# A four-layer graph network on one core: one-hot tiles and first-hop messages shared with ScalarE, whole-row loads in a Chebyshev pass, and a zero row per partition

## What is computed

```python
# layer 0: attention diffusion, 4 heads, 5 hops
att = segment_softmax(leaky_relu(s_h + s_t + s_r), head_ids)
Z = broadcast(x[:, None, :])                      # [N, 4, 64], every head begins with x
for _ in range(5):
    Z = segment_sum(0.9 * att[:, :, None] * Z[tail_ids], head_ids) + 0.1 * x[:, None, :]
out = Z.reshape(N, 256) @ W_o
# layer 1: four GCN rounds, each with its own norm
# layer 2: Chebyshev, K = 3
def prop(t): return segment_sum(w[:, None] * t[col], row)
T1 = prop(x);  T2 = 2 * prop(T1) - x;  out = x @ W[0] + T1 @ W[1] + T2 @ W[2] + bias
# layer 3: GIN with batch statistics
```

## Time and profile before

| | |
|---|---|
| median of 3 runs | 10540.99 us (10538.47 to 10543.46) |
| profiled execution | 10568.15 us, span 10566.3 us |
| busy in the span | PE 55%, DVE 64%, ACT 27%, POOL 69% |
| granted TensorE clock, mean of the span | 0.698 |

### The profile page before, as it was taken

The page is one execution under the profiler, slowest core; times in us unless marked ns, Lnnn a source line. Parts: engine busy times, 40 slices in busy tenths (PEclk is TensorE's granted clock), DMA queues, the critical chain, the costliest instruction groups (busy, mean ns, idle before and its releaser), DMA issues. The chain is left out here.

```text
span 10566.3 us, 116038 instructions
## 1 busy us (share of the span) xinstructions
PE 5778.3 (55%) x28479; PEld 4118.1 (39%) x28479; DVE 6794.6 (64%) x14079; ACT 2812.3 (27%) x5049; POOL 7336.9 (69%) x7144
## 2 busy tenths in 40 slices
PE   3756999400000000776867786767774668833338
PEld 1453333100000000775656565555553557733326
DVE  8954333385878787996767676878775766622227
ACT  0042222100222222443434453222221332200006
POOL 2654777577777777775767676767776767677764
PEclk9978999755555555887777787777676775555559
DMA  0064333143545454446866676655444999811127
GB/s 14 4 221 137 71 72 74 31 160 115 166 147 166 148 166 151 121 129 163 223 196 221 194 236 197 228 179 146 137 134 119 316 270 116 115 46 46 45 55 278
DMA packets 1350058, 1518.83 MB, mean 144 GB/s; under 512 B 935889, under 2 KB 1057071, under 8 KB 1349818
## 3 DMA queue, kind: packets, MB, share of 16 engines
q1 hardware_dynamic: 1088840, 1253.58, 37.1%
q0 software_dynamic: 252192, 248.44, 13.5%
q10 hardware_dynamic: 8786, 14.21, 0.4%
HBM read 852.44 MB, written 795.02 MB: 156 GB/s over the span
## 5 line engine op out<-in xcount | busy, mean ns | idle before, releaser
L2600 POOL DMA_INDIRECT r_got<-state,comb_src x1176 | 1197.9, 1019 | 367.6 <-issue 349.5
L314 POOL DMA_INDIRECT payload_or_bias_rows<-payload,place x784 | 875.0, 1116 | 483.6 <-issue 254.4
L1816 PE MATMUL hop_ps_into<-hop_out,span_s 128*128 128x256 f32 x8 | 4.9, 714 | 2047.2 <-DVE hop_out L1644 2047.2
L1453 POOL DMA_INDIRECT hop_got<-edges_b,next_col x784 | 825.7, 1053 | 261.6 <-issue 236.3
L1453 POOL DMA_INDIRECT hop_got<-edges_a,next_col x784 | 782.1, 998 | 259.7 <-issue 238.4
L1816 PEld LDWEIGHTS hop_ps_into<-hop_out,span_s 128*128 128x128 f32 x8 | 2.0, 311 | 2049.5 <-DVE hop_out L1644 2049.5
L1712 ACT COPY hop_got<-hop_zeros 128x1792 f32<-128x1792 f32 x224 | 378.2, 1688 | 1107.4 <-DVE hop_ps_msg L1595 1098.6
L1644 DVE SCALAR_TENSOR_TENSOR hop_out<-hop_out,hop_runs_now,hop_ps_msg 128x256 f32<-128x256 f32 x1176 | 565.6, 481 | 51.3 <-DVE hop_ps_msg L1597 0.5
L2882 PE MATMUL r_ps_v<-dense1g,r_gt 128*128 128x128 f32 x3136 | 570.1, 353 | 0.0
L2882 PEld LDWEIGHTS r_ps_v<-dense1g,r_gt 128*128 128x128 f32 x3136 | 516.4, 256 | 127.0 <-issue 127.0
L2700 DVE SCALAR_TENSOR_TENSOR r_acc<-r_acc,r_runs_now,r_got 128x64 f32<-128x64 f32 x1173 | 335.1, 286 | 289.9 <-DMA r_got<-state,comb_src 251.1
(11 more groups left out here) (842 smaller groups left out, 18108.8 us busy)
## 6 DMA issues: line engine op xcount, KB each, us to landing
edges_a<-hop_out SPq DMA_DIRECT2D x112, 896.0 KB
edges_b<-hop_out SPq DMA_DIRECT2D x112, 896.0 KB, 4.3
r_in<-state SPq DMA_DIRECT2D x168, 448.0 KB, 4.6
hop_side<-x_dst SPq DMA_DIRECT2D x280, 224.0 KB, 4.5
own<-plain_y SPq DMA_DIRECT2D x56, 952.0 KB
x_and_sums<-c_y SPq DMA_DIRECT2D x56, 896.0 KB, 5.9
last_in<-x_and_sums SPq DMA_DIRECT2D x56, 896.0 KB
r1a_in<-own SPq DMA_DIRECT2D x84, 448.0 KB, 6.1
```

What stands on the lines that cost most here:

```text
L314: nc.gpsimd.indirect_dma_start(out=t.raw[:, n, :], out_offset=None, in_=t.pay[k], in_offset=bass.IndirectOffsetOnAxis(t.place[:, k, n:n + ...
L1453: pool.indirect_dma_start(out=got[:, u, c, :], out_offset=None, in_=table, in_offset=at, bounds_check=EP - 1, oob_is_err=False).then_inc(g ...
L2600: pool.indirect_dma_start(out=got[:, n, c - b * CT, :], out_offset=None, in_=table, in_offset=bass.IndirectOffsetOnAxis(idx[:, at + c:at + ...
```

## The change

Four places, and numbers that shift payload loads between blocks. In the histogram DVE makes six of seven one-hot tiles. ACT makes the seventh: two squares of (iota - digit)/16, and one Relu(1 - 256 * square), which is 1 at the digit and 0 elsewhere; PE waits for it before the batch's last pair. Two more small DVE instructions prepare `minus` in the sorting block. In hop 0 ACT copies `sides` to PSUM and makes the messages of the last `BY_SCALAR` = 3 columns by 12 small activations; DVE makes those of four columns from the PSUM copy. `cheb_first` loads whole rows of `x2`. `next_col` of an edge with nothing to gather becomes `NONE` + its partition. `EARLY` goes from 240 to 208, `UNDER_DEGREES` from 255 to 222, and 30 payload loads go from hop 0 to the end of hop 4.

```diff
@@ histogram
-                        for n in range(B):
+                        for n in range(B - 1):
@@
+                            if n == B - 1:
+                                pe_.wait_ge(act_ready[k][u], i + 1)
@@
+            for k in range(2):
+                @repeat(act, TURN)
+                def _(i):
+                    for u in range(2):
+                        at = bass.ds((i * 2 + u) * B + B - 1, 1)
+                        nc.scalar.activation(apart[:, u, 0:BLK], t.iota[:, 0:BLK], ACT.Square, scale=NEAR, bias=minus[:, 0, k, at])
+                        nc.scalar.activation(apart[:, u, BLK:], t.iota[:], ACT.Square, scale=NEAR, bias=minus[:, 1, k, at]).then_inc(squared[u], 1)
+                        act.wait_ge(squared[u], k * TURN + i + 1)
+                        wait(act, used[k][u], i)
+                        nc.scalar.activation(oh[:, u, B - 1, :], apart[:, u, :], ACT.Relu, scale=-1.0 / (NEAR * NEAR), bias=t.ones[:, 0:1]
+                                             ).then_inc(act_ready[k][u], 1)
@@ constants
-EARLY = 240
-UNDER_DEGREES = 255
+EARLY = 208
+UNDER_DEGREES = 222
+AFTER_LAST_HOP = 30
+BY_SCALAR = 3
@@ target_fields
-            c.link(nc.vector.tensor_scalar(tmp[:, 0, :], t.row_f[:], float(NP), float(NONE), ALU.is_lt, ALU.mult))
+            c.link(nc.vector.tensor_scalar(spare[:], row[:], float(NONE), None, ALU.add))
+            c.link(nc.vector.tensor_scalar(tmp[:, 0, :], t.row_f[:], float(NP), spare[:], ALU.is_lt, ALU.mult))
@@ edge_pass, SP, DVE, ACT
-                            past(sp, side_scaled if banks else msg_ready, i, u, 2)
+                            past(sp, act_part if begins else side_scaled if banks else msg_ready, i, u, 2)
@@
-                            m = msg[:, u % 2].rearrange("p c (h d) -> p c h d", h=H)
-                            nc.vector.tensor_tensor(m, four(sides[:, u % 2]), att, ALU.mult).then_inc(msg_ready[u], 1)
+                            here = CT - BY_SCALAR
+                            m = msg[:, u % 2, 0:here].rearrange("p c (h d) -> p c h d", h=H)
+                            copied = ps_side[:, u % 2, 0:here * D].rearrange("p (c d) -> p c d", c=here)
+                            att = t.att_e[:, :, bass.ds(order(i, u) * CT, here)].rearrange("p h c -> p c h").unsqueeze(3)
+                            dve.wait_ge(side_scaled[u], i + 1)
+                            nc.vector.tensor_tensor(m, copied.unsqueeze(2).to_broadcast([P, here, H, D]),
+                                                    att.to_broadcast([P, here, H, D]), ALU.mult).then_inc(msg_ready[u], 1)
@@
+                        if begins and c == CT - BY_SCALAR:
+                            dve.wait_ge(act_part[u], i + 1)
@@
+                    if begins:
+                        act.wait_ge(side_in[u], (i + 1) * 16)
+                        past(act, msg_ready, i, u, 2)
+                        nc.scalar.copy(ps_side[:, u % 2, 0:CT * D], sides[:, u % 2].rearrange("p c d -> p (c d)")).then_inc(side_scaled[u], 1)
+                        for c in range(CT - BY_SCALAR, CT):
+                            for h in range(H):
+                                ins = nc.scalar.activation(msg[:, u % 2, c, h * D:(h + 1) * D], sides[:, u % 2, c, :], ACT.Copy,
+                                                           scale=t.att_e[:, h, bass.ds(order(i, u) * CT + c, 1)])
+                        ins.then_inc(act_part[u], 1)
@@ cheb_first
-        in0, put0 = (sb(n, [P, RING, T, D]) for n in ("in0", "put0"))
+        in0, put0 = sb("in0", [P, RING, T, D]), sb("put0", [P, RING, T, D + 1])
@@
-                    sp.dma_start(put0[:, u], nodes(t.x2, i, u)[:, :, 0:D]).then_inc(put0_ok[u], 16)
+                    sp.dma_start(put0[:, u], nodes(t.x2, i, u)).then_inc(put0_ok[u], 16)
@@
-                    nc.vector.tensor_tensor(in0[:, u], in0[:, u], put0[:, u], ALU.add).then_inc(merged[u % 2], 1)
+                    nc.vector.tensor_tensor(in0[:, u], in0[:, u], put0[:, u, :, 0:D], ALU.add).then_inc(merged[u % 2], 1)
```

More of the change, by code:

```diff
@@ L180, in digits, with histogram @@
     link(dve.tensor_copy(hi, tmp))
-def histogram(nc, t, w, lo, hi):
+NEAR = 1.0 / 16.0
+def histogram(nc, t, w, lo, hi, minus):
     B, TURN = CT, TILES // (2 * CT)
@@ L202, in histogram @@
         ps = ctx.enter_context(nc.psum_tensor("hist_ps", [P, 8, 512], F32))
-        ready, used = ([[sem(f"{n}{k}{u}") for u in range(2)] for k in range(2)] for n in ("onehots_ready", "onehots_used"))
+        ready, act_ready, used = ([[sem(f"{n}{k}{u}") for u in range(2)] for k in range(2)]
+                                  for n in ("onehots_ready", "onehots_act_ready", "onehots_used"))
+        apart, squared = sb("onehots_apart", [P, 2, BLK + NBLK], F16), [sem(f"onehots_squared{u}") for u in range(2)]
         zero, begun, chain, pe, stored = (sem(n) for n in ("hist_zero", "hist_begun", "hist_chain", "hist_pe", "hist_stored"))
@@ L286, in _ @@
         def _(act):
+            for k in range(2):
[9 more added lines that the diff above has]
+                                             ).then_inc(act_ready[k][u], 1)
+                for u in range(2):
+                    act.wait_ge(used[k][u], TURN)
             tanh(act)
@@ L547, in sort_edges @@
             wt = c2.enter_context(nc.sbuf_tensor("weights_in", [P, TILES], F32))
[L548 to L549 removed]
+            sort_sources(nc, t, key, wt, lo, hi, minus, (w["src"], w["dst"], w["etype"], w["weight"]))
+        histogram(nc, t, w, lo, hi, minus)
 def add_tensors(nc, ctx, t):
@@ L1350, in edge_pass @@
     banks = kind == "heads" and table is not None
+    begins = kind == "heads" and table is None
     with ExitStack() as ctx:
@@ L1368, in edge_pass @@
         if banks:
-            ps_m, ps_side = psum("ps_msg", [P, 4 * 512]), psum("ps_side", [P, 2, 512])
+            ps_m = psum("ps_msg", [P, 4 * 512])
+        if banks or begins:
+            ps_side = psum("ps_side", [P, 2, 512])
         add = None if rows_too else sb("add", [P, O])
@@ L1401, in edge_pass @@
         linked, blank, added = sem("linked"), sem("blank"), sem("added")
-        runs_ready, side_scaled, zeroed = sems("runs_ready"), sems("side_scaled"), sems("zeroed")
+        runs_ready, side_scaled, zeroed, act_part = sems("runs_ready"), sems("side_scaled"), sems("zeroed"), sems("act_part")
         rt_done, rt_read, gt_done, gt_read, lin_done = sem("rt_done"), sem("rt_read"), sem("gt_done"), sem("gt_read"), sem("lin_done")
@@ L1479, in _ @@
                         scatter(n - lag)
+            if after is not None:
+                payload_rows(nc, t, 1, after, t.got_t)
             if rows_too:
                 return
-            if after is not None:
-                payload_rows(nc, t, 1, after, t.got_t)
             for u in range(RING):
@@ L1578, in _ @@
                         dve.wait_ge(gathered[u], (i + 1) * 16 * CT)
-                    if side is not None and not banks:
+                    if side is not None and not banks and not begins:
                         dve.wait_ge(side_in[u], (i + 1) * 16)
@@ L1826, in attention @@
         a, b = tables[(k - 1) % 2], tables[k % 2]
-        first = TILES - (4 - k) * AFTER_HOP
+        first = TILES - AFTER_LAST_HOP - (4 - k) * AFTER_HOP
         edge_pass(nc, t, f"hop{k}", "heads", t.runs_s, t.span_s, t.fix_edge, table=a, idx=t.next_col, target=b,
@@ L1830, in attention @@
     recycle(nc)
-    edge_pass(nc, t, "hop4", "heads_out", t.runs_s, t.span_s, t.fix_node_s, table=tables[1], idx=t.next_col, target=t.own1)
+    edge_pass(nc, t, "hop4", "heads_out", t.runs_s, t.span_s, t.fix_node_s, table=tables[1], idx=t.next_col, target=t.own1,
+              after=range(TILES - AFTER_LAST_HOP, TILES))
     recycle(nc)
```

15 lines of the change are left out of this document (9 added, 6 removed).

## The result

The changed kernel took **10377.28 us** (median of 4 runs, 10372.00 to 10378.96) against 10539.73 us for the kernel before beside it (4 runs, 10529.54 to 10543.46): a ratio of 0.9845, 95% interval 0.9834 to 0.9857, or -162 us. A second measurement on another chip gave 0.9833 (0.982 to 0.9847). I had said 10302 us and 10270 to 10360: the direction was right, the time lies 17 us above the range.

A forecast was written before the change was run, and what follows sets the result against it. It took DVE to bound the histogram, DVE-slowed POOL hop 0, full DMA and POOL cheb_first, slow one-row reads cheb_second. Terms -46 - 131 + 1 - 10 - 53 = -239 us gave 10302 us from 10540.99; range 10270 to 10360.

The forecast's parts named there:

- What bounds the kernel now: Opening step: DVE bounds the histogram, POOL slowed by DVE hop 0, DMA and POOL cheb_first, slow one-row reads cheb_second.
- Histogram, -46: Histogram: DVE saves one column of seven, 0.44 us for 112 batches, less 3 us for lower clock: -46 us.
- the clock: Rival, histogram: PE at 1.2 GHz would bind, +214 us in place of -46, total 10562 us; chance 3%.
- the tie: Histogram: each batch also waiting 0.1 us would leave a gain of 38 us, the term's lower bound.
- Hop 0, -131: Hop 0: DVE's iteration falls from 5.67 to 4.84 us, POOL's loads run unhindered, side loads are covered: -131 us.
- The rule on the port: Rival, hop 0: L1644's two SBUF inputs keep blocking POOL, gain 60 us or less, total 10373 us; chance 3%.
- ACT bounds hop 0: Rival, hop 0: activations at 0.45 us make ACT's iteration 6.15 us, gain 58 and not 131, total 10375; chance 8%.
- 30 loads behind hop 4, 0: End of hop 4: 30 payload loads moved there fit POOL's idle 44 us, costing 0 us, bound 0 to +4.
- plain_rows +1: plain_rows: 32 and 1 loads moved there from the histogram and the block after it cost +1 us.
- cheb_first, -10: cheb_first: whole-row loads remove small DMA pieces and shorten a DMA backlog at the block's end: -10 us, bounds 0 and 20.
- cheb_second, -53: cheb_second: 128 zero rows instead of one bring the indirect queue's share towards 9.4%: -53 us, bounds 0 and -60.
- I take the sum off each: Final step: subtract -239 us from both the profiled 10568.15 us and the median 10540.99 us, giving 10329 and 10302.

The follow-up runs named there:

- e1: The kernel before the change, unchanged, profiled once more: 10572.66 us (profiled, one run).
- f2: The changed kernel with four one-hot buffers in the histogram instead of two: ratio 0.9812 against the kernel before.
- e3: The changed kernel with four side-row buffers in hop 0 instead of two and each side load issued one iteration earlier: ratio 0.98 against the kernel before.
- g4: The kernel before with only the zero row per partition added: 10504.75 us against 10535.66, ratio 0.9972.
- f1: The changed kernel, unchanged, measured again on another chip: 10367.07 us, ratio 0.9833 against the kernel before.
- e4: The changed kernel with cheb_first's addition of two SBUF tiles written as scalar_tensor_tensor instead of tensor_tensor: ratio 0.9824 against the kernel before.

## Why the prediction missed

By its own steps, in the order of the sum:

- *What bounds the kernel now.* Right for hop 0 and cheb_second, for the histogram in the first profile but not in e1, where POOL ended it. Half right for cheb_first: POOL paces it, but "the DMA backlog shows at the end" was wrong.
- *Histogram, -46: was -39.2.* The price of ACT was right (493, 606 and 835 ns against 0.49, 0.60 and 0.81 us), the clock held (1.00 while the batches ran, but for the start of the second array, as in the kernel before), and I named the tie at 0.1 us a batch as the bound of 38. I took too little of it: it cost 2.71 - 2.565 = 0.145 us a batch, some 16 us over 112. That the term came out only 7 us short is luck, for DVE's own batch is 2.565 us and not 2.63: seven columns took 3.07 in my row but 2.99 in e1, and 6/7 of 2.99 is 2.56. POOL's loads, which the sum doesn't name for this block, are the next bound: they take back 8 of the 20 us that four buffers free in DVE's loop (f2).
- *Hop 0, -131: was -98.8.* Two steps failed. "ACT may run one iteration ahead, so a side load that lands late is covered too" looked at ACT's buffer and not at when SP may issue. SP's list has the load behind the store of two iterations before, so it is issued 0.9 us after DVE's sums of that iteration end, though ACT has released the buffer 3.1 us earlier. It lands 4.1 us later, ACT's copy takes 0.5, and 0.9 + 4.1 + 0.5 = 5.5 us is more than the 4.84 that DVE needs for the iteration between; its iteration came out at 5.30. e3, which moves the load up by one store and gives it four buffers, puts this at 21.6 us. "Then the carry and the block's end as now, 6.6 us" was the other: the drain in it rose by 8.22 - 1.44 = 6.8 us. What is left is some 4 us: in e3 DVE's sums end 277.6 us into the block, where I had 2441 - 2166.5 = 274.5, and POOL's loads, at 1.305 us each and not 1.25, end at 281.6, where I had 265.5.
- *The rule on the port.* The Trainium skill ("SBUF — State Buffer", SBUF: two separate sides) has DVE's two-tile instructions block a GpSimd instruction that reads SBUF. In hop 0 L1680 stands beside loads of 0.94 to 1.20 us, and their mean of 995 ns is 51 over the free 944: some 11 us in the block. So its rival (-60) was wrong in size, but the price isn't nothing, as I had it.
- *ACT bounds hop 0.* Did not happen. An activation of 64 elements comes every 0.24 us, where I had 0.34 as the limit. By the Trainium skill ("ScalarE: Activation LUTs", What ACT_TABLE_LOAD costs) it is 0.24; the trace agrees.
- *30 loads behind hop 4, 0; plain_rows +1.* Right within the scatter (-0.5 us in hop 4's block, -4.8 in that of plain_rows).
- *cheb_first, -10: was +3.7, or nothing.* The tail was a drain, and DMA share isn't what the block is short of.
- *cheb_second, -53: was -52.2* in the trace, and the queue's share fell as said. Without a profile it is -31 (g4).
- *"I take the sum off each".* In the profiles 50 us of the sum were missing: 7 + 32 + 14 + 1 as above, less 4 that the other blocks gave. From 10568.15 to 10378.96 is -189; between the medians it is -162. I took a profiled execution that stood 27 us above the median as a kernel slower everywhere by 0.26%, and carried its block lengths over to the unprofiled runs. That step failed for cheb_second at least: the missing 27 is about the 21 by which g4's ratio and its block in the trace differ. Whether the surplus lay in that block isn't shown: a profile of f1, which has the 128 rows, stood 29 us above its median too. Why the one row costs more in the traces (41 to 52 us) than without (19 to 39) stays open.

So of the 75 us between 10302 and 10377, 7 are the histogram, 28 hop 0's side load and drain, some 10 to 14 cheb_first, and, as an estimate from these differences, 21 to 27 the profiled execution as a base.

## What to carry to other kernels

When a stage gets faster, follow each buffer once round: who must release it before its next load may be issued, what stands ahead of that load in the issuing engine's list and what *that* waits for, and how long the load takes to land. Here the buffer was free 3 us before the load was issued. Producer and consumer within 3% of each other (2.565 and 2.495 us a batch here) on two buffers should be costed with a wait, or given more buffers. Then look at who ends the stage next: here POOL's loads, which didn't end the block of the changed kernel, took back 8 of 20 us. The idle end of a block is to be read instruction by instruction before a price is put on it, and a profiled execution that lies above the unprofiled median may overstate just the term that is to be removed.

## What the runs showed of the hardware

- Many gathers of one and the same 256 B row took 54.8% of the DMA engines' time for 12.94 MB; over 8 or 128 rows of their own, 11.5 and 11.4% for 12.90 MB.
- The drain on POOL at a block's end took 0.22 to 9.21 us where no byte moved beside it any more. In hops 1 to 3 it was 3.15 us, in cheb_first 8.14 and in the GIN pass 7.00 in every profile, and in hop 0 it was 8.22, 0.22 and 1.44 us behind 212, 227 and 242 loads.
- An instruction of DVE with two tiles in SBUF holds up POOL's indirect DMA whether it is a TENSOR_TENSOR or a SCALAR_TENSOR_TENSOR (e4), and one of 0.49 us does so by some 0.05 us on average.
- Instructions that read one tile do it too, in the histogram: beside DVE's TENSOR_SCALARs in fp16 (256 and 392 elements) a load took up to 1.43 us, and 0.94 once they had ended. The mean of the loads was 1061 ns with a batch of seven columns every 3.07 us, and 1313 ns in e1, the same kernel, with one every 2.99; with six columns it was 1058 ns at 2.71 us and 1308 at 2.565 (f2).
